# Second layer's unit rows of seven batches turned to channels in the expert stage, two tiles a unit

## What is computed

```python
# second layer, first block: h has been normalized and modulated
norm = jnp.maximum(jnp.linalg.norm(x, axis=-1, keepdims=True), EPS)
xn = x / norm * scale * gamma
h = jnp.einsum('bnd,ed->bne', xn, W_qkva)
q, kv, a = jnp.split(h, 3, axis=-1)
a = jax.nn.sigmoid(a)
_, y = jax.lax.associative_scan(binop, (a, kv), axis=1)
return q * y
...
# second block
r = jax.nn.sigmoid(jnp.einsum('btc,dc->btd', xr, W_r))
k = jnp.einsum('btc,dc->btd', xk, W_k)
out = r * jnp.einsum('btc,dc->btd', jnp.square(jax.nn.relu(k)), W_v)
```

## Time and profile before

| | us |
|---|---|
| median of 3 runs | 2839.82 (2839.14 to 2845.86) |
| the profiled execution | 2843.74, its span 2841.9 |
| busy in the span | PE 2672.8, PE weight loads 2037.5, DVE 2202.4, ACT 2219.9, POOL 1913.4 |
| mean granted TensorE clock | 0.926 |

### The profile page before, as it was taken

One profiled execution on the slowest core, in us unless ns is written; L12 is line 12 of the kernel. 1 busy time (PEld: TensorE's weight loads), 2 busy tenths in 40 slices (PEclk: granted clock), 3 DMA queues, 4 the chain that ended last, 5 costly groups with the idle time before them and its releaser, 6 DMA issues. The chain is left out here.

```text
span 2841.9 us, 78357 instructions
## 1 busy us (share of the span) xinstructions
PE 2672.8 (94%) x27878; PEld 2037.5 (72%) x27878; DVE 2202.4 (77%) x8352; ACT 2219.9 (78%) x4501; POOL 1913.4 (67%) x2020
## 2 busy tenths in 40 slices
PE   5999999999999999999999999689999999999788
PEld 3777877777777777777777777566666666666644
DVE  5566876776876876876776765699999999999676
ACT  3888888888888888888888887368878777878566
POOL 2787887887887887887887878324455455455134
PEclk7999999999999999999999999878888778878799
DMA  4000000000000000000000100200000000000001
GB/s 110 1 1 1 9 1 1 9 1 1 9 1 1 8 1 1 9 1 1 9 1 1 42 1 2 108 1 0 0 0 0 0 0 0 0 0 0 2 21 39
DMA packets 12272, 27.88 MB, mean 10 GB/s; under 512 B 1592, under 2 KB 6200, under 8 KB 11840
## 3 DMA queue, kind: packets, MB, share of 16 engines
q1 hardware_dynamic: 12096, 25.74, 2.7%
HBM read 17.33 MB, written 8.40 MB: 9 GB/s over the span
## 5 line engine op out<-in xcount | busy, mean ns | idle before, releaser
L316 POOL TENSOR_TENSOR probs_l<-probs,probs_h 128x512 fp32r<-128x512 f32 x1024 | 1302.7, 1294 | 302.6 <-ACT probs_h L412 297.9
L411 ACT ACTIVATE probs<-bank 128x512 f32<-128x512 f32 x1024 | 641.5, 626 | 266.8 <-PE bank L765 173.0
L600 DVE TENSOR_REDUCE maxes<-ring 128x1 f32<-128x512 f32 x1024 | 659.4, 686 | 181.5 <-PE ring L745 180.4
L412 ACT ACTIVATE probs_h<-bank 128x512 fp32r<-128x512 f32 x1024 | 644.1, 629 | 0.0
L764 PE MATMUL bank<-q_hh,k_hl 128*128 128x512 f32 x1024 | 424.5, 415 | 1.8 <-ACT probs_h L412 1.6
L765 PE MATMUL bank<-q_lm,k_h 65*128 65x512 f32 x1024 | 405.8, 396 | 0.0
L775 PE MATMUL obank<-probs_h,x_l 128*128 128x512 f32 x1024 | 404.5, 395 | 0.0
L777 PE MATMUL obank<-probs_h,x_h 128*128 128x512 f32 x1024 | 403.1, 394 | 0.0
L776 PE MATMUL obank<-probs_l,x_h 128*128 128x512 f32 x1024 | 402.4, 393 | 0.0
L745 PE MATMUL ring<-k_hl,q_hh 128*128 128x512 f32 x1024 | 339.6, 412 | 12.0 <-DVE maxes L600 7.3
L1186 ACT ACTIVATE low_hot<-obank 128x512 f16<-128x512 f32 x512 | 297.1, 605 | 54.1 <-PE obank L1431 40.9
(11 more groups left out here) (282 smaller groups left out, 4933.5 us busy)
## 6 DMA issues: line engine op xcount, KB each, us to landing
xt<-in_x SPq DMA_DIRECT2D x8, 512.0 KB, 8.3
x<-out_x SPq DMA_DIRECT2D x1, 4096.0 KB, 12.6
out_x<-x SPq DMA_DIRECT2D x16, 256.0 KB, 2.0
out_x<-xt SPq DMA_DIRECT2D x7, 512.0 KB, 2.6
mod<-out_x SPq DMA_DIRECT2D x3, 512.0 KB, 15.2
spare<-in_w_q SPq DMA_DIRECT2D x2, 512.0 KB, 5.7
spare<-in_w_qT SPq DMA_DIRECT2D x2, 512.0 KB, 7.2
hot_rule<-in_hot_rule SPq DMA_DIRECT2D x1, 1024.0 KB, 8.3
```

The lines of the kernel that those rows point to most:

```text
L316: nc.gpsimd.tensor_tensor(probs_l[:, i, :], probs[:, s % 4, :], probs_h[:, i, :].bitcast(F32), ALU.subtract).then_inc(low_ready, 1)
L411: nc.scalar.activation(probs[:, s % 4, :], st[s % 4], ACT.Exp)
L412: nc.scalar.activation(probs_h[:, i, :], st[s % 4], ACT.Exp).then_inc(st_free[s % 4], 1)
L600: nc.vector.tensor_reduce(maxes[:, i, k:k + 1], ring[bank_of(at)][:], AX.X, ALU.max).then_inc(rows_maxed, 1)
```

## The change

The expert stage gets the turning of the unit rows of batches 0 to 6, a unit of two tiles at a time. `unit_rows` moves ahead of `length_sums` on ACT and writes to a staging tile (`staged`, two tiles of the free `spare_a`) instead of in place; PE turns them in the new `turn_units(u - 2)` ahead of the turn of h, into the second half of `h_bank`; ACT copies them back to hc, now with channels on partitions, in the new `unit_channels` behind hcT. Four tiles of a half lie side by side in hc, so that the second layer's products read them directly. Gamma and the root of the width go into the weights once (`w_scaled`), by DVE. Only batch 7 is still turned in the second layer.

```diff
@@ build_experts
-        scratch = spare_b
+        staged, scratch = spare_a[:, 0:2], spare_b
@@ scalar
                 for q in range(2):
                     row = hc[:, bass.ds(2 * u + q, 1), :].rearrange("p o d -> p (o d)")
-                    nc.scalar.activation(row, row, ACT.Copy, scale=roots[:, 2 + q:3 + q])
+                    last = nc.scalar.activation(staged[:, q], row, ACT.Copy, scale=roots[:, 2 + q:3 + q])
+                last.then_inc(units_staged, 1)
+
+            def unit_channels(u):
+                nc.scalar.activation(hc[:, bass.ds(2 * u, 2), :], h_bank[:, 2 * P:4 * P].rearrange("p (q d) -> p q d", q=2), ACT.Copy)
...
                 exponentials(u + 1)
+                if not (isinstance(u, int) and u < 3):
+                    unit_rows(u - 3)
                 if not (isinstance(u, int) and u < 2):
                     length_sums(u - 2)
                 if not (isinstance(u, int) and u < 1):
                     means(u - 1)
-                if not (isinstance(u, int) and u < 3):
-                    unit_rows(u - 3)
-                if not (isinstance(u, int) and u < 1):
                     square_sums(u - 1)
                 centred(u + 2)
+                if not (isinstance(u, int) and u < 3):
+                    unit_channels(u - 3)
                 coarse_shares(u + 1)
...
+            nc.scalar.sem_inc(units_staged, 3)
...
             unit_rows(PAIRS - 5)
+            act.wait_ge(turned_h, PAIRS + 1)
+            unit_channels(PAIRS - 5)
             coarse_shares(PAIRS - 1)
@@ tensor
             def turn_h(u):
                 if not (isinstance(u, int) and u == 0):
                     pe.wait_ge(hT_ready, u)
+                if not isinstance(u, int):
+                    turn_units(u - 2)
...
+            def turn_units(u):
+
+                pe.wait_ge(units_staged, u + 1)
+                for q in range(2):
+                    mm = nc.tensor.transpose(h_bank[:, (2 + q) * P:(3 + q) * P], staged[:, q], ident[:])
+                return mm
...
             expert_weights(PAIRS - 2)
+            pe.wait_ge(hT_ready, PAIRS)
+            turn_units(PAIRS - 2).then_inc(turned_h, 1)
             turn(PAIRS - 1)
@@ build_second_layer
-        gamma_s = sb("l1_gamma", [P, 1])
+        w_scaled = sb("l1_w_scaled", [P, 3 * D])
@@ scalar
-            def turned_units(b, k):
-                act.wait_ge(turned, 2 * b + k + 1)
-                nc.scalar.activation(xnT[:, half(k)], ring[k][:], ACT.Copy, scale=gamma_s[:]).then_inc(xnT_ready, 1)
+            def last_turned(k):
+                act.wait_ge(turned, k + 1)
+                nc.scalar.activation(xnT[:, half(k)], ring[k][:], ACT.Copy).then_inc(xnT_ready, 1)
...
+                if b + 1 == B - 1:
+                    last_turned(0)
                 if scanning:
-                    turned_units(b + 1, 0)
                     decays(b + 1, 0)
-                    turned_units(b + 1, 1)
+                if b + 1 == B - 1:
+                    last_turned(1)
@@ vector
-            nc.vector.tensor_scalar(gamma_s[:], cols[:, 0:1], ROOT_D, None, ALU.mult).then_inc(consts_ready, 1)
+            nc.vector.tensor_scalar(w_scaled[:], w_qkva[:], cols[:, 0:1], ROOT_D, ALU.mult, ALU.mult).then_inc(consts_ready, 1)
@@ tensor
-            def turn_units(b, k):
-                if b == B - 1 and k == 0:
+            def turn_last(k):
+                if k == 0:
                     pe.wait_ge(last_steps, 9)
-                if b:
-                    pe.wait_ge(x_scanned, 2 * b - 1 + k)
-                turn(ring[k], lambda i: units[:, b * TB + 4 * k + i]).then_inc(turned, 1)
+                pe.wait_ge(x_scanned, 2 * (B - 1) - 1 + k)
+                turn(ring[k], lambda i: units[:, (B - 1) * TB + 4 * k + i]).then_inc(turned, 1)
...
-                    pe.wait_ge(xnT_ready, 2 * b + k + 1)
+                    if b == B - 1:
+                        pe.wait_ge(xnT_ready, k + 1)
+                        channels = xnT[:, half(k)]
+                    else:
+                        channels = units[:, some(b, k)].rearrange("p t d -> p (t d)")
+                    if b and j == 2:
+                        pe.wait_ge(x_scanned, 2 * b - 1 + k)
...
-                    nc.tensor.matmul(bank(k), w_qkva[:, j * D:(j + 1) * D], xnT[:, half(k)], start=True, stop=True).then_inc(full, 1)
+                    nc.tensor.matmul(bank(k), w_scaled[:, j * D:(j + 1) * D], channels, start=True, stop=True).then_inc(full, 1)
...
+            pe.wait_ge(consts_ready, 1)
             for b in range(-1, B + 1):
...
-                if scanning:
-                    turn_units(b + 1, 0)
+                if b + 1 == B - 1:
+                    turn_last(0)
...
-                if scanning:
-                    turn_units(b + 1, 1)
+                if b + 1 == B - 1:
+                    turn_last(1)
```

More of the change, by code:

```diff
@@ L1073, in build_experts @@
         h_ready = sem("l1_h4_ready")
+        units_staged = sem("l1_units_staged")
         code_ready = sem("ex_code_ready")
@@ L1807, in gates @@
                 nc.scalar.activation(rgate[:, half(k)], obank[1][:], ACT.Sigmoid).then_inc(rgate_ready, 1)
-            act.wait_ge(consts_ready, 1)
             for b in range(-1, B + 1):
```

## The result

The changed kernel takes **2861.72 us** (median of 4 runs, 2858.71 to 2863.07) beside 2842.03 of the kernel before on the same chip: ratio 1.0059, 95% interval 1.0047 to 1.0071. It is slower by about 0.6% (the medians lie 19.7 us apart, and the interval of the ratio is 13 to 20 us); forecast were 2840.0 and "the two ends cancel". The profiled execution took 2863.07 with a span of 2861.3, 19.4 more than before.

| stretch | before | after | difference | forecast |
|---|---|---|---|---|
| up to the last turn of h in the loop (L1408, now L1419) | 2631.19 | 2650.92 | +19.7 | +6.8 |
| from there to the second layer's first instruction on DVE | 65.99 | 70.64 | +4.7 | 0 |
| second layer | 144.7 | 139.7 | -5.0 | -6.6 |

What follows compares the result with a forecast made beforehand. It took PE's own order to set the pace of three expert units in four, DVE close behind. Expert stage +6.8 and second layer -6.6 gave +0.2 on 2843.74, put on the median as 2840.0 us; range 2834 to 2847.

Steps and rivals of the forecast that it cites:

- the two ends cancel: Whole kernel: the expert stage's loss and the second layer's gain leave the total within 0.3%, +0.2 us; chance 0.80.
- Step 1: Expert stage, PE ahead of the turn of h: two more transposes per unit, 0.35 us each unit that pays, +6.8 in all.
- the return moves along: Expert stage, PE: the full clock's return shifts with the transposes, so a unit pays the full 0.47 us instead of 0.35.
- Slower: the transposes hold the clock down too: Rival, PE behind every `expert_weights`: price 14.1 us with the fourth units, total +10.3, 2850 us; chance 0.10.
- Slack absorbed by the first unit behind a fourth one: Expert stage: a wait that ACT and DVE end there absorbs part of the delay, 1.25 us over six units.
- Step 2: Expert stage, where PE waits already: the fourth unit's wait for hcT hides its transposes, with 0.5 us to spare.
- Step 3: Expert stage, ACT: one more copy per unit, 256 wide, fits into idle time ahead of the shares; cost 0.
- Step 4: Second layer's start: the first scans no longer wait for a queued copy, -4.2 us, and the next batch gains -0.8.
- The half clock, taken at 0: Second layer's start: PE, less densely busy, may stay at half clock longer, costing 0 to 2.8 us; taken as 0.
- Step 5: Second layer's steady batches: a batch falls from 14.76 to 14.32 us, bound by ACT's nine operations; -1.6 in all.
- The rival that DVE is the true pace: Expert stage: most of PE's 0.47 is eaten, total -8.4, 2831 us; chance 0.10, shared with a larger second-layer start gain.
- the change doesn't free the second layer: Rival, second layer's start: scaled weights or the previous batch's sum come late, losing 1 to 3 us, 2842; inside the forecast's 0.80.

Runs made afterwards that it cites:

- e6_no_copy: As e3_tail, but ACT doesn't copy the turned unit rows back, leaving them unused: 2857.65 us, ratio 1.0056 to the kernel before.
- e3_tail: The changed kernel with ACT's last copy of unit rows moved behind the shares, the ids and their turn: 2857.31 us, ratio 1.0052 to the kernel before.
- e1_layer2: The kernel before with only the changed second layer, its expert stage as before: 2839.65 us, ratio 0.9987 to the kernel before.
- e5_no_turns: As e3_tail, but without the expert stage's transposes, ACT copying the staging tile itself: 2838.17 us, ratio 0.9986 to the kernel before.
- e8_gap: As e3_tail, but the two transposes stand behind the turn of h, where PE waits for hcT: 2836.93 us, ratio 0.9982 to the kernel before.

## Why the prediction was wrong

**Step 1, the two transposes, is the term that failed**, mis-sized by a factor of three: +6.8 forecast with ends +4.3 and +10.8, +19.7 measured up to the last turn of h. The mechanism was named: they run at 1.2 GHz with no cover (0.48 from pair to pair, 0.47 forecast) and "the return moves along". But I took "the return moves along" as the upper end, at the transposes' own 0.47, and the middle, 0.35, as the price. It isn't an end. The full clock came back later than by the delay, at the end of the second L1434 instead of inside it and often later still, so old work ran at the half clock too. In numbers of one batch: PE's busy time is up by 101.49 - 97.67 = 3.8 us, of which 1.9 are the transposes as they run, at the half clock, and 1.9 old work that takes longer; its idle time is down by 8.15 - 7.73 = 0.4, all of it in the fourth unit (1.14 + 1.43 for 2.98); in sum +3.4, as measured. The granted clock agrees as far as its two digits go: time at the half clock up from 2 x 0.19 x 105.8 = 40.2 to 2 x 0.22 x 109.2 = 48.0 us, an estimate. At half a us each that is +3.9, with the transposes' work at full clock, 1.0, it is +4.9, 1 us over the 3.8, which the second digit of the clock leaves open. The forecast had 3 x 0.35 = 1.05 for a batch, no more than the transposes' work at full clock. "Slower: the transposes hold the clock down too" was the right rival as to the clock, and its price, 14.1, was short as well, for the same reason (products in place of the transposes gave batches of the same length). The bounds had been made from the inserted work alone, while the half clock touches everything that PE does until it returns.

**Slack absorbed by the first unit behind a fourth one**, -1.25: in late batches nothing was absorbed, the interval behind the first is 26.55 us in place of 25.32. The trace before had a sign of this. In the unit where L1465 came 0.46 later, the second pair of L1416, read in the normal unit as 1.35, took longer:

```profile
2210.16 2.02 PE L1416 MATMUL obank<-w_eff,hcT 128*128 128x512 f32 x2
```

A delay of 0.46 had thus been followed by 0.67 more on the next product. I took the delay as slack and didn't read on. The sentence on what would be wrong, batches "over 107.5 (the clock)", is what came: 109.2.

**Step 2.** That the fourth unit hides its transposes was right. PE's wait for hcT is 1.43 in place of 2.98, where about 0.6 was forecast: the step measured its spare time to the start of hcT (2180.85), but the product starts at 2181.44, 1.1 behind the turn's forecast end, and ACT reaches hcT 0.23 later now (3.04 us behind the exponentials for 2.81). PE waits there 1.14 for the staged rows, as the step's own time for them (2179.0) implies; "no wait of PE for L1231" in the list of what the profile would show contradicts it and was wrong. "The last pair lies under PE's wait of 0.96 us" was wrong by 4.7 us: I had looked for the cover of the transposes on PE and not at the copy that waits for them on ACT, with the shares queued behind it. 3.1 of it is shown to be that queue; the other 1.6 go when the pair goes or stands behind the turn of ids.

**Step 3**, the copy at 0: right, `e6_no_copy` gives the same time as `e3_tail` (2857.65 and 2857.31).

**Step 4**, the start: -3.94 for -4.2; the scaling took 0.42, 0.56 forecast. The next batch gave -0.60 for -0.8. **The half clock, taken at 0**, wasn't: one stretch moved into a batch (18.08 for about 16.5) and one out of the last, and where it lies in the start decides how much that gains. In `e1_layer2` the start took 29.34, 1.27 longer with the same instructions at the same granted clock of 0.94; its stretch at the half clock lies 6 us later and falls on the first product of the mixing, a pair of which takes 1.02 us at full clock:

```profile
2719.96 1.91 PE L1999 MATMUL obank<-mix_now,w_rkv 128*128 128x512 f32 x2
```

In the changed kernel the stretch falls right behind a wait of 2.85 us of PE and costs nothing, for `e3_tail`, whose start has the full clock throughout (1.00), takes 28.07 as well. `e5_no_turns` and `e8_gap` take 29.36 and 29.34. So the -3.94 that agrees with the forecast is in part luck: in three of these five traces the start gained 2.7. In the changed kernel the moves into and out of a batch cancel, by luck too.

**Step 5** was too large. The loop through the turn of mixed and ACT's mixes did take over (the chain of waits runs through ACT's nine operations, 2788.37 to 2794.38), but it is 14.43 and 14.55, not 14.32, and batch 7, still turned, takes 14.99 instead of 14.77. In `e1_layer2`, where these four intervals have a granted clock of 1.00, they (16.49, 14.42, 14.54, 14.99 for 16.83, 14.76, 14.76, 14.77) gain 0.68, not 1.6. Over the whole second layer, the changed kernel's -5.0 is the high end: `e1_layer2`, `e3_tail`, `e5_no_turns` and `e8_gap` take 140.7 to 141.2, 3.6 to 4.0 less than before.

The rival that DVE is the true pace is out: the batch grew by 3.4 us at 102.7 us of DVE's work in place of 102.6, and DVE's wait at the slot ids more than doubled. That the change doesn't free the second layer is out too.

## What to carry to other kernels

An instruction put ahead of a product that PE reaches at the half clock isn't priced by its own duration: what it pushes back is the moment at which the full clock returns, and old work pays too. A place at full clock is cheaper, but wasn't free either: 1.7 us a batch for 0.9 of work. Look for a wait of PE that is there anyway and as long as the insertion, even one of 0.65 us directly behind: that place cost nothing. A consumer that is put into an in-order queue must be checked against the time of what it waits for, above all in the last turn of a loop, where the producer comes late.

## What the runs showed of the hardware

- A loop and PE's clock can fall into step. Without added work or with it in a gap the late batches are 105.82 us; with two, three, four or six transposes or two products ahead they are 109.22 to 109.26, though PE's inserted time differs by up to 0.85 us a unit (0.48 to 1.33). With one transpose the length repeats over three batches (320.85), with two in `combine` over two (215.04). That the clock is what ties them together is read from the granted clock and the longer products; no run holds the clock fixed.
- The time is then no measure of the work: six transposes cost 7 us more than two, and taking two of six out would have seemed to be worth 1 us, no more than the noise.
- A product of 128 columns in f32 with the identity held PE for 0.51 us at the half clock where a transpose of the same tile held it 0.24.
- A tensor_scalar 128x384 in f32 with a column and a constant took DVE 0.42 us.
